# Third stretch of a two-layer decoder kernel: norm rows and a polynomial on other engines, sums in PSUM banks, another weaving of the score matmuls

## The reference, cut to what matters

```python
x = x + L0_ffn(layernorm(x))                        # here: the gather of its rows
x = x + L1_attn(layernorm(x))                       # 16 heads of 16, causal, adaptive temperature
x = x + L1_xattn(layernorm(x), ctx, phi)            # one head, scores + coef * phi
h = rmsnorm(layernorm(x)); q, k = rope(h @ wq), rope(h @ wk)   # L1_ffn, its attention: causal, 16 heads
... top-2 routing to 8 experts, whose work is the fourth stretch

# adaptive temperature, for each row of each head:
p = softmax(logits); H = sum(-p * log(p + 1e-9))
poly = -0.037*H**4 + 0.481*H**3 - 2.3*H**2 + 4.917*H - 1.791
beta = where(H > 0.5, max(poly, 1), 1)
p = softmax(logits * beta)
```

## Time and profile before

| what | us |
|---|---|
| median of 3 runs (1640.0 to 1643.1) | 1640.1 |
| profiled execution, time | 1647.2 |
| profiled execution, span | 1645.4 |
| PE busy / its weight loads | 1345.9 / 1006.8 |
| VectorE busy | 881.0 |
| ScalarE busy | 663.7 |
| GpSimd busy | 451.2 |
| third stretch, first and last instruction | 706.6 to 1370.0 |

### The profile page before, as it was taken

The page is one execution under the profiler, slowest core; times in us unless marked ns, Lnnn a source line. Parts: engine busy times, 40 slices in busy tenths (PEclk is TensorE's granted clock), DMA queues, the critical chain, the costliest instruction groups (busy, mean ns, idle before and its releaser), DMA issues. The chain is left out here.

```text
span 1645.4 us, 22721 instructions
## 1 busy us (share of the span) xinstructions
PE 1345.9 (82%) x8381; PEld 1006.8 (61%) x8419; DVE 881.0 (54%) x2038; ACT 663.7 (40%) x1197; POOL 451.2 (27%) x422
## 2 busy tenths in 40 slices
PE   6888898983999999955778886988878753999993
PEld 4565575752999999933455564665556432666662
DVE  3575767672111111148878889889775322333333
ACT  3454655551323232224456665666564321222220
POOL 1113030302000000068644545636451202111112
PEclk9999999995999999976699899999989766999997
DMA  8563361701777778230000000000004121111114
GB/s 319 231 160 98 95 159 59 195 3 50 258 266 265 264 266 318 86 103 29 11 4 11 7 4 11 33 4 11 27 1 189 58 80 52 43 45 44 43 35 154
DMA packets 65164, 168.36 MB, mean 102 GB/s; under 512 B 7464, under 2 KB 42162, under 8 KB 54944
## 3 DMA queue, kind: packets, MB, share of 16 engines
q1 hardware_dynamic: 51088, 138.10, 25.9%
q0 software_dynamic: 6528, 16.09, 2.9%
q10 hardware_dynamic: 7440, 12.71, 2.1%
HBM read 123.64 MB, written 45.06 MB: 103 GB/s over the span
## 5 line engine op out<-in xcount | busy, mean ns | idle before, releaser
L936 ACT ACTIVATE b_ht<-ps,b_b 128x154 f32<-128x154 f32 x256 | 85.1, 387 | 197.2 <-PE ps L903 183.5
L1979 PE MATMUL ps<-experts,d_xt 128*128 x320 | 153.3, 603 | 1.6 <-ACT d_xt L1965 1.6
L951 DVE TENSOR_SCALAR b_yt<-ps,b_b 128x154 f32<-128x154 f32 x64 | 21.3, 374 | 238.8 <-PE ps L916 238.8
L903 PE MATMUL ps<-b_xet,ring 128*128 128x154 f32 x1024 | 142.3, 296 | 1.1 <-DVE b_xet L944 1.1
L916 PE MATMUL ps<-b_ht,ring 128*128 128x154 f32 x1024 | 139.7, 294 | 0.4 <-DVE b_yt L951 0.4
L903 PEld LDWEIGHTS ps<-b_xet,ring 128*128 128x128 f32 x1024 | 137.0, 191 | 1.2 <-DVE b_xet L944 1.2
L916 PEld LDWEIGHTS ps<-b_ht,ring 128*128 128x128 f32 x1024 | 136.2, 189 | 0.6 <-issue 0.6
L1200 PE MATMUL ps<-cf,experts 128*128 128x128 f32 x512 | 80.6, 311 | 26.1 <-ACT experts L1268 25.8
L1235 DVE TENSOR_REDUCE c_mx<-ps 128x8 f32<-128x1024 f32 x64 | 77.4, 1211 | 38.4 <-PE ps L1188 31.6
L1949 POOL DMA_INDIRECT y<-d_yd,d_to x40 | 39.4, 984 | 212.7 <-DVE d_yd L2036 212.7
L1200 PEld LDWEIGHTS ps<-cf,experts 128*128 128x128 f32 x512 | 68.2, 162 | 38.5 <-ACT experts L1268 34.8
(11 more groups left out here) (307 smaller groups left out, 2833.6 us busy)
## 6 DMA issues: line engine op xcount, KB each, us to landing
ring<-in_w SPq DMA_DIRECT2D x64, 1024.0 KB, 5.7
xd<-zero SPq DMA_DIRECT2D x6, 3120.0 KB
a_kp<-in_ctx_k SPq DMA_DIRECT2D x8, 1024.0 KB, 5.7
experts<-in_wd SPq DMA_DIRECT2D x1, 7552.0 KB
d_xd<-xd SPq DMA_DIRECT2D x40, 130.0 KB, 2.1
xe<-zero SPq DMA_DIRECT2D x1, 4928.0 KB, 28.3
b_xe<-xe SPq DMA_DIRECT2D x32, 154.0 KB
ye<-b_ye ACTq DMA_DIRECT2D x32, 154.0 KB
```

Of the source, the lines that this page charges most:

```text
L903: r = pe.matmul(ps[:, b, CAP * (m % 2):CAP * (m % 2) + CAP], w1r[:, slot, k, P * m:P * m + P], xet[:, e % 2, k, :], start=(k == 0), stop=( ...
L936: r = a.activation(ht[:, e % 2, m, :], ps[:, b, CAP * (m % 2):CAP * (m % 2) + CAP], ACT.Gelu, bias=b1[:, e, m:m + 1])
L1979: m = pe.matmul(ps[:, b, :], xt[:, j % 2, k, :], w13[:, bass.ds(e, 1), at:at + F1], start=(k == 0), stop=(k == KD - 1))
```

## The change

Six things change in the third stretch, and one number for its memory:

- **Norm rows.** `n0r`, `n1r`, `n2r` and the second norm's `n2m` are done by ScalarE as `scale * x + shift`; GpSimd works out `shift = -mean * root` with two more steps (`norm_scale_shift`). In the rotary norm the first rows now wait for the first root alone, and only `n2m` for the second. VectorE loses its calls of `norm_rows` in this stretch; in place of them its statistics wait for the rows of the group before (`mix.xn.at(g - 1)` and the like).
- **Polynomial.** `po` is on GpSimd, ten small operations in place of VectorE's seven, written in even and odd powers, with seven waits on its own semaphore.
- **Sums in banks.** The cross-attention's scores plus `phi` stay in bank 6 through maximum and subtraction, and the rotary products with the sine go back into bank 6 in place of the SBUF tile `rt`.
- **First attention's banks.** The scores of unit u of a group wait only for the copy of unit u of the group before (`pt_in.at(g - 1, u)`), so that they can stand between that group's units. In turn the transposes of unit u wait until the next group's scores of unit u - 1 are read (`dd.at(g + 1, u - 1)`).
- **Last group.** There the second attention puts its odd units into the banks of the first (`apart`, `place`, `other`), and a unit waits for the one two before.
- **Order table.** All numbers of `AT_C` are new.
- `EARLY`, the part of the experts' weights that is loaded at the start of the stretch, is 1024 columns in place of 512, and the `os` tiles lie outside the shared area.

```diff
-EARLY = 512
+EARLY = 1024
...
-def norm_scale(c, t, n, con, again=False):
+def norm_scale_shift(c, t, n, con, again=False):
 
     pool = c.nc.gpsimd
-    var, rs, r2 = t.mv[:, :, 1], t.rs[:, :], t.r2[:, :]
+    mean, var, rs, r2, shift = t.mv[:, :, 0], t.mv[:, :, 1], t.rs[:, :], t.r2[:, :], t.shift[:, :]
     pool.wait_ge(*t.mean.at(n))
+    pool.tensor_scalar(shift, mean, -1.0, None, ALU.mult)
     pool.tensor_scalar(rs, var, 1e-5, None, ALU.add).then_inc(*c.po.up())
     pool.wait_ge(*c.po.now())
-    if not again:
-        pool.tensor_tensor(rs, rs, con["half"], ALU.pow).then_inc(*t.scale.up())
-        return
     pool.tensor_tensor(rs, rs, con["half"], ALU.pow).then_inc(*c.po.up())
     pool.wait_ge(*c.po.now())
-    pool.tensor_tensor(r2, rs, rs, ALU.mult).then_inc(*c.po.up())
+    if again:
+        pool.tensor_tensor(r2, rs, rs, ALU.mult).then_inc(*c.po.up())
+    pool.tensor_tensor(shift, shift, rs, ALU.mult).then_inc(*t.scale.up())
+    if again:
+        pool.wait_ge(*c.po.now())
+        pool.tensor_tensor(r2, r2, var, ALU.mult).then_inc(*c.po.up())
+        pool.wait_ge(*c.po.now())
+        inverse_root(c, r2, con["half"], 1e-5, t.scale2)

+def norm_rows_scalar(c, t, n, x, out, done):

+    a = c.nc.scalar
+    a.wait_ge(*t.scale.at(n))
+    for s in range(GS):
+        m = a.activation(out[:, s, :], x[:, s, :], ACT.Identity, bias=t.shift[:, s:s + 1], scale=t.rs[:, s:s + 1])
+    m.then_inc(*done.up())

...
-    "fetch0": (0, 3.9, 8.7, 15.6, 20.4, 24.3, 47.5, 55.2), "xk": (0, 124, 177.5, 235.2, 290.7, 346.3, 407.8, 457.1),
+    "fetch0": (0, 5, 12.8, 19.2, 30.3, 153.8, 206.2, 208.7), "xk": (0, 121.6, 180.5, 242.6, 297.5, 360, 425.4, 479.9),
...
-        self.os, self.ao = big("os_" + name, [P, 2 * P]), big("ao_" + name, [P, GS, D])

-    def scores(self, c):
-        return c.ps[:, self.b0:self.b0 + 2, :].rearrange("p b (h k) -> p (b h) k", k=P)
+        self.os, self.ao = sb("os_" + name, [P, 2 * P]), big("ao_" + name, [P, GS, D])

+    def apart(self, g):
+        return self.other is not None and g == NG - 1

+    def place(self, g, u):

+        return self.other if self.apart(g) and u % 2 else self

+    def scores(self, c, g, u):
+        b0 = self.place(g, u).b0
+        return c.ps[:, b0:b0 + 2, :].rearrange("p b (h k) -> p (b h) k", k=P)
 
 
...
     def scores(u):
         s, ch = UNITS[u]
+        b0 = l.place(g, u).b0
         yield at("sc", u)
         if u == 0:
             pe.wait_ge(*l.q_in.at(g))
             pe.wait_ge(*l.k_in.at(g))
+        if woven:
+            if u:
+                pe.wait_ge(*l.dd.at(g, u - 1))
             if g:
-                pe.wait_ge(*l.pt_in.at(g - 1))
-        else:
-            pe.wait_ge(*(l.dd if ahead else l.pt_in).at(g, u - 1))
+                pe.wait_ge(*l.pt_in.at(g - 1, u))
+        elif u == 1 and l.apart(g):
+            pe.wait_ge(*l.other.pt_in.at(g))
+        elif u or g:
+            pe.wait_ge(*earlier(l.pt_in, g, u, 2 if u and l.apart(g) else 1))
         for b in range(2):
-            pe.matmul(ps[:, l.b0 + b, :], con["ident_bf"], con["mask"], start=True, stop=True, skip_group_check=True)
...
-        if ahead:
-            pe.wait_ge(*(l.pt_in.at(g, u - 1) if u else l.dd.at(g)))
+        if woven and u == 0:
+            pe.wait_ge(*l.dd.at(g))
+        elif woven:
+            pe.wait_ge(*l.pt_in.at(g, u - 1))
+            if g + 1 < NG:
+                pe.wait_ge(*l.dd.at(g + 1, u - 1))
         for h in range(NU):
-            m = pe.transpose(ps[:, l.b0 + h // 4, P * (h % 4):P * (h % 4) + P], d[:, h, :], con["ident"])
...
-        if g or u:
-            pe.wait_ge(*earlier(l.ao_in, g, u, 1))
+        if u == 1 and l.apart(g):
+            pe.wait_ge(*l.other.ao_in.at(g))
+        elif g or u:
+            pe.wait_ge(*earlier(l.ao_in, g, u, 2 if u and l.apart(g) else 1))
...
-        two = Attention(c, sb, "2", (3, 4, 5), 2, shared)
+        two = Attention(c, sb, "2", (3, 4, 5), 2, shared, one)
...
-                yield at("po", u)
-                v.wait_ge(*hr.at(g, u))
-                v.tensor_scalar(gt[u][:, :], h, -0.5, None, ALU.is_lt)
-                v.tensor_scalar(p, h, POLY[0], None, ALU.mult).then_inc(*c.dv.up())
-                for q in (-POLY[1], POLY[2], -POLY[3]):
-                    v.wait_ge(*c.dv.now())
-                    v.scalar_tensor_tensor(out=p, in0=p, scalar=q, in1=h, op0=ALU.add, op1=ALU.mult).then_inc(*c.dv.up())
-                v.wait_ge(*c.dv.now())
-                v.scalar_tensor_tensor(out=p, in0=p, scalar=POLY[4], in1=gt[u][:, :], op0=ALU.add, op1=ALU.mult).then_inc(*c.dv.up())
-                v.wait_ge(*c.dv.now())
-                v.tensor_scalar(p, p, 1.0, None, ALU.max).then_inc(*be.up())
...
+                yield at("po", u)
+                pool.wait_ge(*hr.at(g, u))
+                pool.tensor_tensor(sq_h, h, h, ALU.mult).then_inc(*c.po.up())
+                pool.tensor_scalar(g_h, h, -0.5, None, ALU.is_lt)
+                pool.wait_ge(*c.po.now())
+                pool.tensor_scalar(p, sq_h, POLY[0], POLY[2], ALU.mult, ALU.add)
+                pool.tensor_scalar(odd, sq_h, -POLY[1], -POLY[3], ALU.mult, ALU.add).then_inc(*c.po.up())
+                pool.wait_ge(*c.po.now())
+                pool.tensor_tensor(p, p, sq_h, ALU.mult)
+                pool.tensor_tensor(odd, odd, h, ALU.mult).then_inc(*c.po.up())
+                pool.wait_ge(*c.po.now())
+                pool.tensor_tensor(p, p, odd, ALU.add).then_inc(*c.po.up())
+                pool.wait_ge(*c.po.now())
+                pool.tensor_scalar(p, p, POLY[4], None, ALU.add).then_inc(*c.po.up())
+                pool.wait_ge(*c.po.now())
+                pool.tensor_tensor(p, p, g_h, ALU.mult).then_inc(*c.po.up())
+                pool.wait_ge(*c.po.now())
+                pool.tensor_scalar(p, p, 1.0, None, ALU.max).then_inc(*be.up())
...
-            v.scalar_tensor_tensor(out=dd, in0=phi[g % 2][:, :, :], scalar=coef[:, 0:1], in1=ps[:, MIX, 0:GT].rearrange("p (s t) -> p s t", s=GS),
+            v.scalar_tensor_tensor(out=at_bank, in0=phi[g % 2][:, :, :], scalar=coef[:, 0:1], in1=at_bank,
                                    op0=ALU.mult, op1=ALU.add).then_inc(*c.dv.up())
             v.wait_ge(*c.dv.now())
-            v.tensor_reduce(m4[:, :], dd, AX, ALU.max).then_inc(*c.dv.up())
+            v.tensor_reduce(m4[:, :], at_bank, AX, ALU.max).then_inc(*c.dv.up())
             v.wait_ge(*c.dv.now())
-            v.tensor_tensor(dd, dd, m4[:, :, None].to_broadcast([P, GS, P]), ALU.subtract).then_inc(*xd_in.up())
+            v.tensor_tensor(dd, at_bank, m4[:, :, None].to_broadcast([P, GS, P]), ALU.subtract).then_inc(*xd_in.up())
             yield at("xz")
...
-            v.tensor_tensor(pair(rt[0:n64, 0, :]), pair(ps[n64:2 * n64, MIX, 0:GT]), of(3, slice(n64, 2 * n64)), ALU.mult).then_inc(*c.dv.up())
+            v.tensor_tensor(pair(ps[0:n64, MIX, GT:2 * GT]), pair(ps[n64:2 * n64, MIX, 0:GT]), of(3, slice(n64, 2 * n64)), ALU.mult).then_inc(*c.dv.up())
             v.wait_ge(*c.dv.now())
-            v.tensor_tensor(kr[0:n64, :], kr[0:n64, :], rt[0:n64, 0, :], ALU.add).then_inc(*kr_in.up())
+            v.tensor_tensor(kr[0:n64, :], kr[0:n64, :], ps[0:n64, MIX, GT:2 * GT], ALU.add).then_inc(*kr_in.up())
...
-            v.tensor_tensor(units(rt), bank, wide(1), ALU.mult).then_inc(*c.dv.up())
+            v.tensor_tensor(bank, bank, wide(1), ALU.mult).then_inc(*c.dv.up())
             v.wait_ge(*c.dv.now())
-            v.tensor_tensor(two.qt[:, :, :], two.qt[:, :, :], rt[:, :, :], ALU.add).then_inc(*two.q_in.up())
+            v.tensor_tensor(units(two.qt), units(two.qt), bank, ALU.add).then_inc(*two.q_in.up())
...
-            at = tick(g)
+            at, xn = tick(g), x_rot[g % 2]
+            yield at("n2r")
+            if g >= 2:
+                a.wait_ge(*xadd.at(g - 2))
+            norm_rows_scalar(c, rot, g, xg_of(g), xn, c.ac)
+            yield at("n2m")
+            a.wait_ge(*rot.scale2.at(g))
+            a.wait_ge(*c.ac.now())
+            if g:
+                a.wait_ge(*rot.turned.at(g - 1))
+            for s in range(GS):
+                m = a.activation(x_rms[:, s, :], xn[:, s, :], ACT.Copy, scale=rot.r2[:, s:s + 1])
+            m.then_inc(*rot.xn.up())
             yield at("xt3")
```

98 lines of the change are left out of this document (50 added, 48 removed), and 183 rows, old and new, of the table AT_C.

## The result

The changed kernel takes **1590.7 us** (median of 4 runs, 1585.9 to 1599.3), the kernel before beside it 1641.6 us (4 runs): ratio 0.9696, 95% interval 0.9652 to 0.9739. That is 51 us, 3%, less; 43 less had been forecast. The profiled execution has a span of 1588.7 us.

The account below looks back on a forecast made before the run. The prediction took the middle to be paced by bank 6's chain of handovers, stretched by queues on VectorE and ScalarE. Middle -23, opening -8 and close -12 made -43 us from the 1640.1 median: 1597 us, range 1568 to 1632.

Parts of the forecast that it names:

- the opening: First two groups of the third stretch: a third of the 24.5 us leaving VectorE is gained, -8 us (0 to -20).
- the close: End of the third stretch: two bank sets bring pairs of heads from 9.8 to 6.3 us apart, -12 us (-7 to -18).
- The middle: Six groups of the third stretch: PE becomes the bound at 90%, 59.9 us per group, -23 us (bounds 0 and -43).
- 74 us off VectorE: Middle: polynomial 44.1, norm rows 25.6 and sum 4.4 us removed; VectorE falls from 52.9 to 40.5 us per group.
- the added wait: A pair's transposes wait until the next group's first-attention scores are read; costed at nothing because the order puts those scores ahead.
- no form of one size taking several durations: Sign expected in the profile after, with VectorE near 380 us in the third stretch.
- At nothing: Third-stretch items costed at zero: unblocked sums in banks, the experts' loads, the added wait, the fetches moved back.
- rival (c): Slower: the added wait stalls PE at 21 places, eating the gain of 43 us from 2.0 us mean stall; chance 0.06.
- waits of 2 us and more ahead of the first attention's transposes: Sign on PE in the third stretch that would show the forecast wrong.
- (a): VectorE's queues were the whole trouble: middle -43, opening -15, close -16, together -74, 1566 us; chance 0.15.
- (b): Nothing gained in the middle, ScalarE's queueing replaces VectorE's; only close and opening pay, -15, 1625 us; chance 0.16.
- (d): GpSimd's small operations are dear: above 0.68 us each the middle is no faster, about 1640 us; chance 0.03.

## Why the prediction was right, point by point

**The time.** 1590.7 us against 1597 (1568 to 1632), -51 against -43. That the sum came out so close is in part luck. The three terms speak of the third stretch, and there the traces show -60.8: 18 us more than forecast, nearly all of it in the opening and the close. In the medians the gap shrinks to 8, since outside the third stretch the profiled run of the change is 4.1 us longer and the profiled run before stood 5.6 us above its median. And the reason for the largest term is only half of the truth.

**The middle**, -23 forecast, -21.3 measured; 60 us between residual sums forecast, 60.2 measured; PE at 90%, measured 89%. The 90% was a choice between 84 and 95 and hit. The step that failed is the reason: the argument was that queues on VectorE stretch the chain through bank 6 and that taking 74 us off VectorE shortens it; the order had no part in this. With the old order the same relief made the middle 6 us longer; with the new order and no relief it was 24 longer; together they are 45 us faster than the new order alone. The order table, of which I weighed only the added wait and the fetches, is half of the change. That its ticks fit the place and length of the moved work is shown for one place, the exponential behind the product with beta; the table, the wait rule and the moved fetches were not tried apart, so which of them the moves need stays open. Within the new order the parts come back as rows 28, sums 15, polynomial 10 us, 53 against 45 for all together, with up to 5.8 and 7.3 us of unnamed waits in the first two.

**VectorE**: 40.5 us per group forecast, 44.1 measured. What I didn't see is that with the fetches the table also moved their sums: 16 of them, 16.4 us or 2.7 per group, stand in the middle now. The other 0.9 is in how I added: the durations of VectorE's rows overlap at their ends, 338.6 us of rows in 317.4 us of busy time before and 280.6 in 264.3 after. By rows the account closes, 338.6 - 74.1 + 16.4 = 280.9; by busy time less than 74.1 us was taken off. The sign "no form of one size taking several durations" did not come either, as the sums show.

**GpSimd** 44.7 forecast, 43.5 measured, with 2.7 us for a polynomial forecast and 2.66 measured. The total is close because two errors cancel: I counted the waits between the ten operations as busy, which they are not (7.8 us per group of busy time where I put 10.8), and left out the issues of the 14 fetches that came into the middle (13.9 us, 2.3 per group). **ScalarE** 42.5 and 42.5, a half row at 0.59 us where I took 0.5. The estimate of 585 ns by the Trainium skill's page ScalarE: Activation LUTs, section "What ACT_TABLE_LOAD costs", was nearer than mine; the trace has 592 to 596.

**At nothing** I put the sums in banks beyond their 4.4 us. Without them the middle is 14.8 us longer, so this term was mis-sized. Two more of these operations than I listed are stretched in SBUF, which makes 8.0 us of VectorE's rows; the long groups are those with unnamed waits of ScalarE, 7.3 us in all. How much of the 14.8 is owed to bank 6 is not shown. The added wait cost 1.0 us in the middle, as I put it. In the opening it held PE 6.2 us in two waits of 3.1. That is what rival (c) gave as its reason, and by my own sign, waits of 2 us and more ahead of the first attention's transposes, I would have been wrong there; the opening got shorter all the same.

**The opening**, -8 forecast, -15.0 measured, a term that was mis-sized. The new order alone gave nothing there (164.0), the moves alone cost 14 (178.2); it is the two together. The rows are 10.2 of it. And GpSimd's polynomial takes some of it back: with eight of its ten operations left out the opening is 6.3 us shorter still.

**The close**, -12 forecast, -24.5 measured: mis-sized, mechanism right. The split last group is 20.3 of it. I took 6.3 us per pair, PE's time at the clock of 0.70; at 1.00 PE needs 15.9 / 4 = 4.0 us, and the pairs came every 4.0 in the mean, where I had expected 6 to 7. I had named a higher clock as a possible extra and given it next to nothing in the sum.

**The rivals.** Of (a), the opening came as it had it (-15) and the close went beyond it (-16); its middle did not come, which ended at 60 us per group. Nor did (b). Its point, that VectorE's relief would buy nothing in the middle, holds in the old order. (c) is excluded in the middle by the 1.0 us row; in the opening its wait is there, at 6.2 us in place of the 43 that it needed. (d) is excluded by 0.2 us per small operation.
